# Softmax exponentials over two PSUM banks, done as one ScalarE instruction or as two of one bank each

## The reference, cut to what matters

```python
# first attention, per head, x normalised; mask is strictly lower triangular and multiplies the scores
att = jnp.einsum('bhqe,bhke->bhqk', q, k) / jnp.sqrt(jnp.float32(he))
att = jax.nn.softmax(att * mask, axis=-1)
out = jnp.einsum('bhqk,bhke->bhqe', att, v)
out = out.transpose(0, 2, 1, 3).reshape(b, c, d) @ Wr + br
x = x + out
# second attention, causal
scores = jnp.einsum('bqhd,bkhd->bhqk', q, k) * scale
scores = jnp.where(causal[None, None], scores, -jnp.inf)
attn = jax.nn.softmax(scores, axis=-1)
ctx = jnp.einsum('bhqk,bkhd->bqhd', attn, v).reshape(B, S, E)
x1 = _layer_norm(x + ctx @ out_proj_w.T + out_proj_b, ln1_w, ln1_b)
# then gates, top 2 of 8 experts, their sum, a last layer norm, and x + that
```

## Time and profile before

| | |
|---|---|
| median of 3 runs | 811.14 us (808.7 to 813.13) |
| the profiled execution: its time, and its span | 811.19 us, 809.4 us |
| PE, ACT, DVE, POOL busy | 675.6, 631.3, 412.3, 325.1 us |
| first to last exponential | 32.3 us to 738.0 us |
| exponentials (L1281) | 576, busy 598.6 us |

### The profile page before, as it was taken

One profiled execution on the slowest core, in us unless ns is written; L12 is line 12 of the kernel. 1 busy time (PEld: TensorE's weight loads), 2 busy tenths in 40 slices (PEclk: granted clock), 3 DMA queues, 4 the chain that ended last, 5 costly groups with the idle time before them and its releaser, 6 DMA issues. The chain is left out here.

```text
span 809.4 us, 15701 instructions
## 1 busy us (share of the span) xinstructions
PE 675.6 (83%) x5752; PEld 283.5 (35%) x5752; DVE 412.3 (51%) x1115; ACT 631.3 (78%) x665; POOL 325.1 (40%) x635
## 2 busy tenths in 40 slices
PE   3589988898898978988998889898878889898644
PEld 2334333333333333333343334233323234334533
DVE  4465352355453742484465643635524533755875
ACT  1389989999797996998898899897798988985000
POOL 3162226323532433532753346425542245534233
PEclk9799999999899998999999999999999999999756
DMA  5766367445655344333464424431473433310000
GB/s 136 264 207 221 96 208 271 138 127 177 202 199 189 131 161 114 114 106 105 136 198 157 157 83 147 124 113 67 134 223 125 139 98 129 97 64 1 26 27 15
DMA packets 76994, 109.81 MB, mean 136 GB/s; under 512 B 13784, under 2 KB 28256, under 8 KB 76896
## 3 DMA queue, kind: packets, MB, share of 16 engines
q1 hardware_dynamic: 73232, 107.85, 41.9%
q10 hardware_dynamic: 3664, 0.77, 0.5%
HBM read 60.91 MB, written 47.68 MB: 134 GB/s over the span
## 5 line engine op out<-in xcount | busy, mean ns | idle before, releaser
L1281 ACT ACTIVATE probs<-scores,shift 128x1024 f32<-128x1024 f32 x576 | 598.6, 1123 | 94.9 <-PE scores L1107 90.1
L1357 POOL TENSOR_SCALAR_AFFINE_SELECT probs<-probs 128x256 f32<-128x256 f32 (+1 forms) x448 | 200.6, 465 | 366.2 <-ACT probs L1281 365.6
L1136 PE MATMUL acc<-probs,v 128*9 128x512 f32 (+3 forms) x3072 | 319.2, 503 | 1.3 <-ACT num L1224 1.0
L1107 PE MATMUL scores<-qs,ks 32*128 32x512 f32 (+3 forms) x1536 | 158.8, 428 | 59.0 <-ACT probs L1281 57.1
L1107 PEld LDWEIGHTS scores<-qs,ks 32*128 32x128 f32 x1536 | 72.3, 187 | 211.1 <-ACT probs L1281 139.4
L1136 PEld LDWEIGHTS acc<-probs,v 128*9 128x9 f32 x3072 | 58.9, 100 | 96.3 <-issue 64.7
L1397 DVE TENSOR_TENSOR prod<-side,G 128x512 f32<-128x512 f32 x47 | 32.5, 691 | 86.9 <-PE side L1089 81.5
L1089 PE MATMUL side<-we,x1T 128*128 128x256 f32 x188 | 66.7, 438 | 4.4 <-DVE prod L1397 4.4
L1089 PEld LDWEIGHTS side<-we,x1T 128*128 128x128 f32 x188 | 28.9, 192 | 49.0 <-issue 27.0
L1338 POOL TENSOR_TENSOR moe<-psum 128x256 f32<-128x256 f32 x32 | 24.7, 770 | 48.1 <-DVE x1b L1397 29.4
L1224 ACT ACTIVATE num<-acc 128x512 f32<-128x512 f32 x64 | 38.5, 601 | 6.5 <-PE scores L1010 4.3
(11 more groups left out here) (177 smaller groups left out, 638.2 us busy)
## 6 DMA issues: line engine op xcount, KB each, us to landing
ks<-k_dram SPq DMA_DIRECT2D x96, 256.0 KB, 4.2
q_dram<-part SPq DMA_DIRECT2D x64, 256.0 KB, 3.1
qs<-q_dram SPq DMA_DIRECT2D x64, 256.0 KB, 3.2
num_dram<-num SPq DMA_DIRECT2D x60, 256.0 KB, 3.1
k_dram<-part SPq DMA_DIRECT2D x32, 256.0 KB, 3.6
xrow<-in_x SPq DMA_DIRECT2D x16, 256.0 KB, 4.4
nat<-num_dram SPq DMA_DIRECT2D x15, 256.0 KB
rdenb<-rden_dram SPq DMA_DIRECT2D x15, 256.0 KB
```

The costliest lines, as they stand in the source:

```text
L1107: ins = pe.matmul(scores[:, pair(g, h // 2), h % 2, col:col + w], ks[u][r, kt // TH, (kt % TH) * P:(kt % TH + 1) * P], qs[u][r, q0:q0 + w] ...
L1136: ins = pe.matmul(acc[h * VW:h * VW + VC, q0:q0 + w], v9[V_OF[k]][:, kt, :, HG * hg + h], src, start=(s == 0), stop=last, skip_group_check ...
L1281: act.activation(dst, src, ACT.Exp, bias=shift[:, column(k):column(k) + 1], scale=SCALE).then_inc(probs_raw, 1)
L1357: ins = pool.affine_select(out=blocks, in_=blocks, compare_op=ALU.is_ge, fill=0.0, base=a - 1, pattern=[[0, blocks.shape[1]], [1, P]], cha ...
```

## The change

Each exponential unit, one instruction of 128 x 1024 (two banks), becomes two of 128 x 512 (one bank each), one behind the other. Both have the same bias column and scale. The waits stand ahead of the first; the second alone raises `probs_raw`, so the others are told once per unit, as before. In a half set each of the two takes the first halves of two banks.

```diff
@@ -1271,14 +1271,15 @@
                 act.wait_ge(scores_ready, g + 1)
                 if n >= NPB:
                     act.wait_ge(group_done, GROUP_OF[n - NPB] + 1)
-                if len(UNITS_OF[g]) == 1:
-                    low_, high = sorted((pair(g, 0), pair(g, 1)))
-                    src = scores[:, low_:high + 1:high - low_, :, 0:HALF // 2]
-                    dst = probs[n % NPB][:, :, :].rearrange("p a (c s) -> p a c s", c=2)
-                else:
-                    src = scores[:, pair(g, n - FIRST_UNIT[g]), :, :].rearrange("p c s -> p (c s)")
-                    dst = probs[n % NPB][:, :, :].rearrange("p c s -> p (c s)")
-                act.activation(dst, src, ACT.Exp, bias=shift[:, column(k):column(k) + 1], scale=SCALE).then_inc(probs_raw, 1)
+
+                for c in range(2):
+                    if len(UNITS_OF[g]) == 1:
+                        src = scores[:, sorted((pair(g, 0), pair(g, 1)))[c], :, 0:HALF // 2]
+                        dst = probs[n % NPB][:, c, :].rearrange("p (c s) -> p c s", c=2)
+                    else:
+                        src, dst = scores[:, pair(g, n - FIRST_UNIT[g]), c, :], probs[n % NPB][:, c, :]
+                    ins = act.activation(dst, src, ACT.Exp, bias=shift[:, column(k):column(k) + 1], scale=SCALE)
+                ins.then_inc(probs_raw, 1)
                 while e < NP and evacuated(e) <= n:
                     evacuate(e)
                     e += 1
```

## The result

The changed kernel takes **870.08 us** (median of 4 runs, 861.12 to 873.47) against 809.92 us before (4 runs, 806.88 to 813.13): a ratio of 1.0734, 95% interval 1.0679 to 1.0789, slower. The profiled execution took 871.34 us with a span of 869.5. Some executions of this program run in a slower state; the ratios leave them out, and a median can hold one.

The account below looks back on a forecast made before the run. ACT and PE, each 88 to 89% busy in the stage of exponentials, were taken to bound the kernel together. 811.19 us plus 59 (89 more on ACT less 30 hidden) gave 870 us, range 850 to 888.

Parts of the forecast that it names:

- What bounds: In the stage of exponentials ACT and PE, each 88 to 89% busy, hand work to each other; neither bounds alone.
- The price of an instruction: On ACT, 576 more instructions' fixed cost: +0.155 us a unit, 89 us in all, exponentials of 512 columns spaced 0.578.
- How much is hidden: ACT's idle time where PE is late takes up 30 us of the 89; the remaining 59 us shows.
- 63 gaps: ACT's waits for scores put down to PE's lateness, 64 us in all; each gives back 0.47 us, 30 us together.
- round trip: ACT's wait behind a half set for scores PE starts only then: mostly 0.21 us, 56 times, 12 us, staying unchanged.
- rival D: PE's clock: lower busy share brings ten more half-clock stretches, 25 us on top of 870, so 895 us; chance 0.08.
- The rest: Signs in the profile after: tail 71 us, ACT's gaps about 45 us, PE's waits for exponentials some 90 or more.
- A: PE's gaps all filled, so PE takes nearly all: stage 716 + 12 = 728 us, +22, 833 us; chance 0.07.
- B: Nothing is hidden; the delay goes once round the loop between ACT and PE: +89, 900 us; chance 0.06.
- C: The fixed part of ACT's instruction is larger, +0.22 us a unit: +85, 896 us; chance 0.06.
- E: Faster: a pair takes 0.96 us, ACT gains 23 us, 803 us, if spacing is under 0.50 us; chance 0.03.

Follow-up runs that it names:

- run 12: The changed kernel run once more, unchanged, for a second profile: 870.07 us, the profiled execution 864.53 us.
- run 6: The changed kernel with each of a unit's two instructions taking 256 columns of both banks: 870.26 us.
- run 1: The kernel before with only the first unit of each two-unit group (256 of 576) split in two: 832.47 us, ratio 1.0297.
- run 2: The kernel before with only the second unit of each two-unit group split in two: 835.73 us, ratio 1.0323.
- run 9: Run 7 with the one-column exponential raising the signal, so it stands ahead of the signal and not behind it: 884.41 us, ratio 1.0862.
- run 3: The kernel before, units whole, with the bias column left out of the exponentials (softmax shift not applied): 792.33 us, ratio 0.9798.
- run 4: The changed kernel, units split, with the bias column left out of the exponentials (softmax shift not applied): 802.43 us, ratio 0.9922.
- run 5: Every unit done as four instructions of 256 columns: 1038.59 us, ratio 1.2844 against the kernel before.
- run 7: The kernel before with a further one-column exponential, with bias, behind each whole unit and its signal: 870.2 us, ratio 1.0783.
- run 8: The kernel before with part of a pass's first scores begun before the half set's exponential is done; every third half set split: 808.1 us, ratio 0.9968.

## Why the prediction came out right

*What bounds.* Right. The stage alone changed, and both ACT and PE had a say in it.

*The price of an instruction.* Right in kind, 8 us too high in size: 0.140 us a unit by spacing where 0.155 was taken, 81 us for 89; ACT's busy time grew by 82. The slope that mattered, 0.83 ns a column, is between the bounds of the earlier trace rows and close to the 0.825 chosen; but the spacing then is 0.57 and not 0.578.

*How much is hidden.* Too high as well: 20 us for 30 in the first profile, 25 and 24 in those of runs 12 and 6. The step that failed is 63 gaps that give back 0.47 us each. The working told the gaps apart by size: what was 0.21 was a round trip, and what was 0.43 or more was PE's lateness and would shrink. But the round trip shows in full, 0.70 us, wherever no copy fills it, and those gaps stayed. By place there were 63 gaps at the starts of passes (34 us, not 12) and 56 others (42 us, not 64), and the 56 gave back 0.34 to 0.41 us each. With 56 gaps of 0.47 the working would have had 26 us. What it also left out is PE's clock, the mechanism of rival D, which was priced as all or nothing at 25 us on top. PE's busy time rose by 20 us with 79 us of half clock in the stage where it had been 42. Over whole executions the mean went from 84 us (the 45 of the kernel before) to 116 (eight with the changed kernel's ACT work: its own, runs 6 and 12); 32 us at 0.27 is 9 us of the 60, as an estimate. How the shortfall is shared between these two causes stays open.

So the price was 8 us too high and the hidden part 5 to 10 us too high, and the two cancelled. That was luck; the 870 was met more exactly than its terms deserved.

*The rest.* The tail stayed and ACT's gaps went to 52 us for "about 45". PE's waits went to 107 for "some 90 or more". The granted clock of the stage, 0.95, stayed above the 0.93 named for D.

*The rivals.* A and B were off by 37 and 30 us. A's own floor was wrong too: with 34 us of round trips in place of 12, its stage would be 750 us and not 728. B's reason, that latency round the loop decides, falls with runs 1 and 2, though run 9 shows that it counts at the starts of passes. C falls with the spacing of 0.57, and the smaller slope behind it has a cause now: a one-column instruction costs more than the line through the larger sizes gives. E falls on its own condition, a spacing under 0.50 us. Runs 3 and 4 show why: the bias column is paid by each instruction.

The Trainium skill's page "ScalarE: Activation LUTs", section "What ACT_TABLE_LOAD costs", gives the split a price of 0.187 us a unit. The slope (0.833 ns) and the operand's 93 ns agree with runs 3 to 5; the spacing it gives for 512 columns, 0.61 us, does not: 0.569 was measured, and the measurement decides.

## What to carry to other kernels

A ScalarE instruction over two PSUM banks should not be cut in two unless somebody uses the earlier end: each cut costs the fixed part (0.14 us here with a bias column), on an engine that shares the bound three quarters of it showed (62 of 82 us), and idle time in the same stage is no proof that there is room. Read spacing from starts, not durations, and put work that must be added behind the signal that others wait for, not ahead of it. An estimate of what idle time absorbs should sort the gaps by their place in the program, not by their size: a round trip absorbs nothing that stands ahead of the signal, and the same round trip left 0.21 us in one place and 0.70 in another.

## What the runs showed of the hardware

- Back-to-back exponentials with a bias column start every 0.142 us + 0.833 ns a column: 0.356 at 256 (run 5), 0.569 at 512, 0.996 at 1024 (run 7; the median before is 0.998). Without the column it is 0.09 us less: 0.477 and 0.903 (runs 4 and 3). At one column the line doesn't hold: 0.185 with (run 7) and 0.09 without, 0.04 over it.
- Durations in a train grow while the spacing stays. In run 9 the whole exponentials from 454 to 456 us and at 465 us:

```profile
453.91 1.11 ACT L1282 ACTIVATE probs<-scores,shift 128x1024 f32<-128x1024 f32 x1
...
455.09 1.12 ACT L1282 ACTIVATE probs<-scores,shift 128x1024 f32<-128x1024 f32 x1
...
463.84 1.17 ACT L1282 ACTIVATE probs<-scores,shift 128x1024 f32<-128x1024 f32 x1
465.02 1.17 ACT L1282 ACTIVATE probs<-scores,shift 128x1024 f32<-128x1024 f32 x1
```

  1.18 us from one to the next at either place, 1.11 us long at first and 1.17 later. A longer duration is not a slower engine.
- Two 32-row score products cost PE as much time as four side by side, 0.50 us (run 8).
- Among 45 executions of one and the same program the span went with PE's time at half clock, 0.27 us for each us (run 12).
